# A linear-attention retrieval stage: features repeated by TensorE matmuls instead of 32 SBUF copies

## The chip, the cores and the metric

One NeuronCore of one Trainium2 chip runs the whole kernel. The metric is the device time of one execution in microseconds (us), from the first to the last instruction of that core and what lies around them. Before the change it is 643.27 us, the median of 3 runs (642.25 to 644.81).

## What is computed

The kernel is a two-layer network over 1024 tokens (32 sequences of 32) with 256 features: attention, gated networks with adapters, and in the second layer a retrieval from banks of memories, paged attention and a mixture of experts. The change lies in the retrieval (`_L1_attn_ref` in the reference), cut here to what is kept of it:

```python
sigma_q = elu(q) + 1                      # q = hidden @ Wq.T, 16 heads of 16 features
a_unnorm = einsum('bhsd,nhde->nbhse', sigma_q, memories)      # 4 banks n
norm     = einsum('bhsd,nhd->nbhs', sigma_q, memory_norms)
a = a_unnorm / clip(norm, 1e-6)[..., None] * active[n]
combined = einsum('nbhse,hn->bhse', a, softmax(bank_weights))
out = combined @ Wo.T                     # added to x
```

The kernel divides first and then multiplies by the memories: for every head, bank and token there is one share, softmax weight times active over norm. The features of a pair of heads (32 rows), repeated for 4 banks (128 rows), are multiplied by their shares, and one matmul with 128 rows of memories sums over banks and features at once.

## The kernel before, around the retrieval

All activations are kept features by tokens: two chunks `c` of 128 features, 1024 tokens in two halves `n` of 512 columns. There is no scheduler. Each engine has a list of instructions written out by hand (`lin_tensor`, `lin_vector`, `lin_scalar`, and SP's list of DMAs), which it takes in order, and semaphores are what one waits for of another. The retrieval stands between the second attention (`att_b`) and the paged attention (`page_*`).

1. TensorE projects `yT` with `lin_wq` into PSUM banks 4 to 7 (L1093); VectorE and ScalarE make `sig` = elu + 1 of it (L1154, L1191, L1147), four blocks (c, n).
2. SP issues 32 DMAs (L1883), each of which copies 32 rows of `sig` over 1024 tokens, 128 KB, to one of four row groups of `sig4`, so that `sig4[:, i]` holds head pair i four times. The 16 of chunk 0 signal `lin_rep0`, those of chunk 1 `lin_rep1`.
3. TensorE makes the norms: 64 rows (4 banks of 16 heads) for each half (L1099). VectorE clips, inverts and scales them on 64 partitions, one half after the other (L1161, L1163, L1166). ScalarE makes a high part of them for the fast fp32r format (L1195), VectorE the rest (L1168).
4. For 16 units (pair i, half n), TensorE spreads the shares from 64 rows to 128 with a 0/1 matrix `sel_r`, two fp32r matmuls a unit (L1117) into four rotating banks; VectorE multiplies by `sig4` into `sigq`, a ring of eight buffers (L1175); after each four units TensorE multiplies by the memories, four matmuls of 32 output rows each (`memories`, L1107), and ScalarE keeps the result as `comb` (L1198).
5. TensorE projects with `lin_wo` (L1127) and VectorE adds into `xT` (L1180). `page_tensor` waits for the four of these (`lin_out` >= 4), and VectorE's part of the page stage stands behind them in its list.

Meanwhile GpSimd gathers 40 blocks of the cache by indirect DMA (L1920), with nothing of the retrieval in its list. SP, after the 32 copies, waits for the last L1175 (`lin_scaled` >= 16), loads the experts' weights of 6.5 MB into `wbig`, over `sig4` (L1886), and then stores the new keys and values (`new_kv`, L1890), for which GpSimd's second series of gathers waits.

A matmul of fp32 operands is in the trace two records, each of which streams the columns twice; one of fp32r operands is one record.

## Time and profile before

| | us |
|---|---|
| median of the runs (lowest, highest) | 643.27 (642.25, 644.81) |
| span of the profiled execution | 644.2 |
| TensorE busy with matmuls | 508.7 |
| VectorE busy | 372.4 |
| retrieval, from the first L1093 to the first matmul of the page stage | 72.8 (328.46 to 401.26) |

The profiled execution is one run; its span is 0.9 us (0.14%) over the median, within the spread of the runs, so differences worked out in it are taken off the median as they are. In the rows, "start us, us" are the start from the beginning of the span and the length of a merged stretch, `x8` the number of instructions in it, and the bracket tells how long the engine was idle before and what released it. "Remote" as a releaser means that the signal came at a time at which no instruction of the trace ended. A granted clock (PEclk) of 1.00 is TensorE's 2.4 GHz, 0.50 is 1.2 GHz.

### The profile page before, as it was taken

How to read it: one execution, taken by the hardware profiler on the slowest of the kernel's cores; microseconds unless marked ns; L12 is line 12 of the kernel's file. 1: busy time of each engine (PE TensorE's matmuls, PEld its weight loads, DVE VectorE, ACT ScalarE, POOL GpSimd, SP SyncE). 2: the span in 40 equal slices, each digit the busy share in tenths (PEclk: the TensorE clock that was granted, in tenths of full speed). 3: DMA queues.
4: the chain of work that ended last, by engine and by line, in shares of the span. 5: the costliest groups of instructions: out<-in, count | busy, mean ns of one | idle time of the engine just before them, and what ended most of it. 6: DMA issues, size and time to landing. Idle time of an engine off the chain costs nothing.

```text
span 644.2 us, 10575 instructions
## 1 busy us (share of the span) xinstructions
PE 508.7 (79%) x4069; PEld 369.7 (57%) x4069; DVE 372.4 (58%) x784; ACT 235.2 (37%) x510; POOL 268.1 (42%) x248
## 2 busy tenths in 40 slices
PE   2978799999998999998775519737889896169975
PEld 1445458886886878666432204625667565068865
DVE  2736667886786887647647205975567564223321
ACT  6024854442433333325820000543456441024330
POOL 4013735463442333145647740088661102715560
PEclk9979699999998999998697558957989787669997
DMA  4990044000000000010029826611010000298416
GB/s 155 404 389 4 2 135 122 1 1 1 0 1 0 1 1 1 1 52 2 1 67 240 216 65 245 236 39 26 16 27 1 3 1 21 103 301 268 135 59 196
DMA packets 26337, 57.00 MB, mean 88 GB/s; under 512 B 4829, under 2 KB 17298, under 8 KB 25392
## 3 DMA queue, kind: packets, MB, share of 16 engines
q1 hardware_dynamic: 19936, 45.06, 20.6%
q0 software_dynamic: 6352, 11.26, 6.2%
q8 instruction: 33, 0.54, 0.3%
q14 instruction: 16, 0.13, 0.1%
HBM read 45.28 MB, written 12.37 MB: 90 GB/s over the span
## 4 chain that ended last, share of the span: by engine, by line
PE 29%; DVE 7%; issue 7%; POOL 3%; another core or an unknown queue 3%; DMA 2%; ACT 1%; DVEq 0%; SPq 0%; POOLq 0%; ACTq 0%
PE ps L1708 4%; PE ps L1322 4%; POOL sorted L1790 2%; PE ps L1716 2%; PE ps L1319 2%; PE ps L1332 1%; PE ps L1381 1%; PE ps L1734 1%; PE ps L403 1%; DVE work L1270 1%; PE ps L1093 1%; PE ps L1127 1%; PE ps L1697 1%; PE ps L691 1%
## 5 line engine op out<-in xcount | busy, mean ns | idle before, releaser
L691 PE MATMUL ps<-x_split,gate_up_split 128*128 128x512 f32 x408 | 103.0, 396 | 0.5 <-ACT work L1802 0.5
L691 PEld LDWEIGHTS ps<-x_split,gate_up_split 128*128 128x128 f32 x408 | 77.3, 190 | 19.1 <-issue 2.4
L884 POOL TENSOR_TENSOR gate_up_split<-wbig,gate_up_split 128x768 fp32r<-128x768 f32 (+1 forms) x25 | 44.5, 1781 | 67.1 <-ACT gate_up_split L824 66.8
L1920 POOL DMA_INDIRECT work<-new_kv,prepi x40 | 43.3, 1081 | 49.0 <-DMA new_kv<-work 37.9
L890 POOL TENSOR_TENSOR down_split<-wbig,down_split 128x384 fp32r<-128x384 f32 (+1 forms) x25 | 29.4, 1175 | 58.3 <-ACT down_split L831 58.3
L715 PE MATMUL ps<-hidden_split,down_split 128*128 128x512 f32 x168 | 46.5, 407 | 8.6 <-ACT hidden_split L873 6.9
L873 ACT ACTIVATE hidden_split<-work 128x512 fp32r<-128x512 f32 x34 | 21.4, 631 | 72.4 <-DVE work L801 72.4
L1920 POOL DMA_INDIRECT work<-in_cache_dram,prepi x40 | 38.5, 962 | 20.1 <-issue 11.9
L1793 POOL DMA_INDIRECT chosen<-work x31 | 30.6, 987 | 33.2 <-ACT work L1779 19.9
L806 DVE TENSOR_TENSOR hidden_split<-work,hidden_split 128x512 fp32r<-128x512 f32 x34 | 29.9, 880 | 23.1 <-ACT hidden_split L873 23.1
L715 PEld LDWEIGHTS ps<-hidden_split,down_split 128*128 128x128 f32 x168 | 32.2, 194 | 17.7 <-issue 10.7
L595 POOL TENSOR_TENSOR work<-work,prep 128x512 f32<-128x512 f32 x16 | 16.8, 1048 | 56.7 <-DVE prep L481 56.0
L1117 PE MATMUL ps<-shares_split,select 64*128 64x512 f32 x32 | 14.2, 614 | 29.3 <-issue 15.7
L1505 ACT ACTIVATE wmid<-ps,prep 128x160 f32<-128x160 f32 x64 | 24.6, 390 | 25.0 <-DVE prep L1404 16.7
L393 PE MATMUL ps<-work 128*32 128x128 f32 x512 | 24.4, 357 | 8.4 <-ACT work L556 8.4
L556 ACT ACTIVATE work<-work 32x512 f32<-32x512 f32 x48 | 29.9, 624 | 0.9
L1117 PEld LDWEIGHTS ps<-shares_split,select 64*128 64x128 f32 x32 | 9.2, 302 | 36.5 <-issue 34.3
L1790 POOL DMA_INDIRECT sorted<-work,prepi x16 | 16.0, 1001 | 33.2 <-DVE prepi L1661 28.6
L801 DVE TENSOR_TENSOR work<-ps,work 128x512 f32<-128x512 f32 x34 | 23.2, 682 | 11.4 <-PE ps L696 7.5
L1322 PE MATMUL ps<-work 128*128 128x160 f32 x128 | 29.6, 360 | 0.0
L393 PEld LDWEIGHTS ps<-work 128*32 128x32 f32 x512 | 19.5, 138 | 15.3 <-ACT work L556 14.6
L1697 PE MATMUL ps<-small,work 128*128 128x128 f32 x62 | 12.4, 287 | 19.4 <-DMA work<-sorted 19.4
(309 smaller groups left out, 1165.5 us busy)
## 6 DMA issues: line engine op xcount, KB each, us to landing
wbig<-in_wE_dram SPq DMA_DIRECT2D x1, 6528.0 KB, 19.2
wbig<-in_wF_dram SPq DMA_DIRECT2D x1, 4992.0 KB, 21.2
wbig<-work SPq DMA_DIRECT2D x32, 128.0 KB
sorted<-wmid SPq DMA_DIRECT2D x1, 3999.0 KB, 15.5
wbig<-in_wG_dram SPq DMA_DIRECT2D x1, 3072.0 KB, 28.1
work<-in_wE_dram SPq DMA_DIRECT2D x6, 384.0 KB
work<-chosen SPq DMA_DIRECT2D x8, 256.0 KB, 4.7
work<-sorted SPq DMA_DIRECT2D x1, 1935.0 KB, 12.9
```

The costliest lines, as they stand in the source:

```text
L393: mm = nc.tensor.matmul(ps[32 * pr:32 * pr + 32, g % 2, c * P:(c + 1) * P], vpar[:, g, a, 4 * c + pr, :], pdiag[:, g % 2, 4 * pr + 2 * c + ...
L556: nc.scalar.activation(pdiag[q, g % 2, :, q], scor[q, g % 4, :].rearrange("p (h k) -> p h k", h=NH), ACT.Copy).then_inc(s("placed"), 1)
L691: mm = nc.tensor.matmul(o, gus[:, w % 2, a, 2 * m + k, :], xs[:, b, k, n * HALF:(n + 1) * HALF], start=(k == 0 and a == b), stop=(k == KC ...
L715: nc.tensor.matmul(o, dns[:, w % 2, a, c], hs[:, i % 2, 0, :], start=(p == 0 and a == 0), stop=False)
L806: nc.vector.tensor_tensor(hs[:, i % 2, 1, :], hid[:, i % 3, :], hs[:, i % 2, 0, :].bitcast(F32), ALU.subtract).then_inc(s("h_lo"), 1)
L884: nc.gpsimd.tensor_tensor(gus[:, k % 2, 1, 0:self.gu_chunks], self.gate_up[:, :, j * P:(j + 1) * P], gus[:, k % 2, 0, 0:self.gu_chunks].bi ...
L890: nc.gpsimd.tensor_tensor(dns[:, k % 2, 1, 0:self.dn_cols], self.down[:, j, :], dns[:, k % 2, 0, 0:self.dn_cols].bitcast(F32), ALU.subtrac ...
L1322: mm = nc.tensor.matmul(ps[:, 2 + b % 2, a * NKEY:(a + 1) * NKEY], qmask[:, b, 2 * a:2 * a + 2, :, :].rearrange("p g h t -> p (g h t)"), k ...
L1708: mm = nc.tensor.matmul(ps[:, t % 2, m * P:(m + 1) * P], tile_w(t)[:, (2 * m + k) * P:(2 * m + k + 1) * P], x_turned[:, t % 2, k * P:(k + ...
L1790: send(sorted_d, by(placei[:, c, g:g + 1]), rows_of[c][:, g, :], None).then_inc(sem("sent"), 16)
L1793: send(chosen_d, by(tile_x(t)[:, D + 1:ROW]), y_tile[:, t % 8, :], None, bounds_check=2 * T - 1, oob_is_err=False)\
L1920: return nc.gpsimd.indirect_dma_start(dst, None, table, bass.IndirectOffsetOnAxis(ap=rows.bitcast(U32), axis=0), **({} if bound is None el ...
```

## The change

**Features.** The 32 DMAs go. TensorE multiplies 32 rows of `sig` with 32 rows of the constant `token` (1 where row and column agree modulo 32), which gives them four times on 128 rows. A batch (`repeat`, L1097 of the new file) is one block (c, n): four such matmuls, on four row groups of the array (rows 0-31, 32-63, ...), into PSUM banks 0 to 3. ScalarE copies each bank into `sig4` (L1216, 16 copies). From the second batch on each matmul waits for the copy out of its bank.

**Shares.** The norms of both halves go to the 128 partitions of one bank (L1105), and the heads stand in another order, so that the shares of chunk c and half n are 32 rows. VectorE clips, inverts and scales them in one pass. They stay fp32: the split into two fp32r parts goes, with ScalarE's rounding of `select` ahead of `att_b`. The units go in pairs (c = 0 and 1 of one r): `spread` is two fp32 matmuls of 32 rows on two row groups (L1121) into two of the banks 5, 6, 0, 1; one semaphore count stands for a pair, and a pair waits for VectorE to be done with the pair before the last.

**Order.** All of half 0 goes first. `memories(n)` takes eight matmuls at once, and the projection of half 0 stands between the spreads of half 1. `sigq` has 16 buffers instead of 8. The constant `sel` has 512 columns instead of 1024. SP's load of the experts' weights waits for the last `memories` as well.

What TensorE's list is from the first projection to the page stage, before (L1093 projects, L1099 norms, L1117 spreads, L1107 memories, L1127 projects):

```order
L1093 MATMUL ps<-work,wmid 128x512 x8
L1099 MATMUL ps<-work,wmid 64x512 x4
L1117 MATMUL ps<-shares_split,select 128x512 x16
L1107 MATMUL ps<-work,wmid 32x512 x4
L1117 MATMUL ps<-shares_split,select 128x512 x8
L1107 MATMUL ps<-work,wmid 32x512 x4
L1117 MATMUL ps<-shares_split,select 128x512 x8
L1107 MATMUL ps<-work,wmid 32x512 x8
L1127 MATMUL ps<-work,wmid 128x512 x8
```

And after, for the same stretch (L1097 repeats, L1105 norms, L1121 spreads, L1131 memories, L1139 projects):

```order
L1085 MATMUL ps<-work,wmid 128x512 x8
L1097 MATMUL ps<-work,small 128x512 x4
L1105 MATMUL ps<-work,wmid 64x512 x4
L1097 MATMUL ps<-work,small 128x512 x12
L1121 MATMUL ps<-work,small 128x512 x10
L1131 MATMUL ps<-work,wmid 32x512 x8
L1121 MATMUL ps<-work,small 128x512 x2
L1139 MATMUL ps<-work,wmid 128x512 x4
L1121 MATMUL ps<-work,small 128x512 x4
L1131 MATMUL ps<-wbig,wmid 32x512 x8
L1139 MATMUL ps<-work,wmid 128x512 x4
```

The repeating of batches 1 to 3 stands ahead of every spread, and each spread, fp32r and twice before, is now one fp32 matmul.

ScalarE's list for the retrieval, with the semaphores that each waits for, before:

```order
L1185 ACTIVATE prep<-prep 64x4 [waits prep_step]
L1186 ACTIVATE prep<-prep 64x1
L1191 ACTIVATE work<-work 128x512 [waits lin_neg] x2
L1191 ACTIVATE work<-work 128x512 [waits lin_sig,lin_neg] x2
L1195 ACTIVATE shares_split<-work 64x512 [waits lin_scale] x2
L1198 ACTIVATE work<-ps 128x512 [waits lin_mem] x4
```

And after:

```order
L1205 ACTIVATE prep<-prep 128x4 [waits prep_step]
L1206 ACTIVATE prep<-prep 128x1
L1211 ACTIVATE work<-work 128x512 [waits lin_neg] x2
L1211 ACTIVATE work<-work 128x512 [waits lin_sig,lin_neg] x2
L1216 ACTIVATE wbig<-ps 128x512 [waits lin_repeated,ffn_down_done]
L1216 ACTIVATE wbig<-ps 128x512 x3
L1216 ACTIVATE wbig<-ps 128x512 [waits lin_repeated]
L1216 ACTIVATE wbig<-ps 128x512 x3
...
L1220 ACTIVATE work<-ps 128x512 [waits lin_mem] x4
```

The copies stand between the exponentials (L1211) and the keeping of the retrieved values (L1220), in four batches.

The diff, cut to its core (left out are the constants' new layout, the widening of slices from 64 to 128 partitions, and lines that only go):

```diff
-        sigq = [cut(work, a + i * HALF, HALF) for a in (6144, 0) for i in range(4)]
+        sigq = [cut(t, a + i * HALF, HALF) for t, a, n in ((work, 6144, 4), (work, 0, 4), (wbig, NH // 2 * T, 8)) for i in range(n)]
         sig4 = cut(wbig, 0, NH // 2 * T).rearrange("p (i t) -> p i t", i=NH // 2)
         comb = cut(work, 8192, 2048).rearrange("p (c t) -> p c t", c=KC)
         neg = cut(work, 0, 1024).rearrange("p (r t) -> p r t", r=2)
         expo = cut(work, 1024, 1024).rearrange("p (r t) -> p r t", r=2)
-        rnorm = work[0:NBANK * NH, 10240:11264]
-        sel_r = split_buf("select", wmid_at, 0, 1024).rearrange("p (i o) -> p i o", i=NH // 2)
-        rnorms = split_buf("shares_split", work_at, 2048, 2048).rearrange("p (s t) -> p s t", s=2)
+        share = cut(work, 10240, HALF)
...
-        PAIRS = [(4 * c + r, n) for c, n in BATCH for r in range(4)]
+        PAIRS = [(c, r, n) for n in range(2) for r in range(4) for c in range(KC)]
+        UNIT_AT = {unit: u for u, unit in enumerate(PAIRS)}
...
+            def repeat(b):
+
+                c, n = BATCH[b]
+                pe.wait_ge(sem("lin_sig"), LIN.index((c, n)) + 1)
+                for r in range(4):
+                    if b:
+                        pe.wait_ge(sem("lin_rep"), 4 * (b - 1) + r + 1)
+                    q = slice(32 * r, 32 * r + 32)
+                    mm = nc.tensor.matmul(ps[:, r, :], const("token")[q, :], sig[q, c, n * HALF:(n + 1) * HALF],
+                                          start=True, stop=True)
+                mm.then_inc(sem("lin_repeated"), 1)
+
+            repeat(0)
             pe.wait_ge(sem("lin_sig"), 4)
-            for n in range(2):
+            for c in range(KC):
+                for n in range(2):
+                    mm = nc.tensor.matmul(ps[64 * n:64 * n + 64, 4, :], nrc[:, c, :], sig[:, c, n * HALF:(n + 1) * HALF],
+                                          start=(c == 0), stop=(c == KC - 1))
+            mm.then_inc(sem("lin_norm"), 1)
+            for b in range(1, 4):
+                repeat(b)
+
+            def spread(n, r):
+
+                pe.wait_ge(sem("lin_scale"), 1)
+                u = 2 * (4 * n + r)
+                if u >= 4:
+                    pe.wait_ge(sem("lin_scaled"), u - 2)
+                elif u == 2:
+                    pe.wait_ge(sem("lin_rep"), 16)
                 for c in range(KC):
-                    mm = nc.tensor.matmul(ps[0:NBANK * NH, n, :], nrc[:, c, :], sig[:, c, n * HALF:(n + 1) * HALF],
-                                          start=(c == 0), stop=(c == KC - 1))
-                mm.then_inc(sem("lin_norm"), 1)
-
-            def memories(b):
-                c, n = BATCH[b]
-                pe.wait_ge(sem("lin_scaled"), 4 * b + 4)
-                for r in range(4):
-                    mm = nc.tensor.matmul(ps[32 * r:32 * r + 32, 2 * c + n, :], pairs[:, 4 * c + r, :],
-                                          sigq[(4 * b + r) % 8], start=True, stop=True)
-                mm.then_inc(sem("lin_mem"), 1)
-
-            pe.wait_ge(sem("sel_ready"), 1)
-            for u, (i, n) in enumerate(PAIRS):
-                pe.wait_ge(sem("lin_share"), n + 1)
-                if u >= 4:
-                    pe.wait_ge(sem("lin_scaled"), u - 3)
-                for part in range(2):
-                    mm = nc.tensor.matmul(ps[:, 4 + u % 4, :], sel_r[0:NBANK * NH, i, :],
-                                          rnorms[0:NBANK * NH, part, n * HALF:(n + 1) * HALF],
-                                          start=(part == 0), stop=(part == 1))
+                    q = slice(64 * n + 32 * c, 64 * n + 32 * c + 32)
+                    mm = nc.tensor.matmul(ps[:, (5, 6, 0, 1)[(u + c) % 4], :], const("sel")[q, r * P:(r + 1) * P], share[q, :],
+                                          start=True, stop=True)
                 mm.then_inc(sem("lin_spread"), 1)
...
+            def memories(n):
+                pe.wait_ge(sem("lin_scaled"), 8 * n + 8)
+                if n:
+                    pe.wait_ge(sem("lin_comb"), 2)
+                for c in range(KC):
+                    for r in range(4):
+                        mm = nc.tensor.matmul(ps[32 * r:32 * r + 32, (4, 7)[c], :], pairs[:, 4 * c + r, :],
+                                              sigq[UNIT_AT[c, r, n]], start=True, stop=True)
+                    mm.then_inc(sem("lin_mem"), 1)
+
+            def project(n):
                 pe.wait_ge(sem("lin_comb"), 2 * n + 2)
-                for k in range(KC):
-                    mm = nc.tensor.matmul(ps[:, 4 + u, :], lin_wo[:, k, c * P:(c + 1) * P],
-                                          comb[:, k, n * HALF:(n + 1) * HALF], start=(k == 0), stop=(k == KC - 1))
-                mm.then_inc(sem("lin_proj"), 1)
+                for c in range(KC):
+                    for k in range(KC):
+                        mm = nc.tensor.matmul(ps[:, 2 + c, :], lin_wo[:, k, c * P:(c + 1) * P],
+                                              comb[:, k, n * HALF:(n + 1) * HALF], start=(k == 0), stop=(k == KC - 1))
+                    mm.then_inc(sem("lin_proj"), 1)
+
+            for r in range(4):
+                spread(0, r)
+            spread(1, 0)
+            memories(0)
+            spread(1, 1)
+            project(0)
+            spread(1, 2)
+            spread(1, 3)
+            memories(1)
+            pe.wait_ge(sem("lin_out"), 2)
+            project(1)
...
+            dve.wait_ge(sem("lin_norm"), 1)
+            nc.vector.tensor_scalar(share, ps[:, 4, :], 1e-6, None, ALU.max).then_inc(sem("lin_inv"), 1)
+            dve.wait_ge(sem("lin_inv"), 1)
+            nc.vector.reciprocal(share, share).then_inc(sem("lin_inv"), 1)
+            dve.wait_ge(sem("lin_inv"), 2)
+            dve.wait_ge(sem("lin_coef"), 5)
+            nc.vector.tensor_scalar(share, share, coef[:, :], None, ALU.mult).then_inc(sem("lin_scale"), 1)
+
+            def keep_projection(n):
+                for c in range(KC):
+                    dve.wait_ge(sem("lin_proj"), 2 * n + c + 1)
+                    to = xT[:, c, n * HALF:(n + 1) * HALF]
+                    nc.vector.tensor_tensor(to, ps[:, 2 + c, :], to, ALU.add).then_inc(sem("lin_out"), 1)
+
+            for u, (c, r, n) in enumerate(PAIRS):
+                dve.wait_ge(sem("lin_spread"), u // 2 + 1)
+                dve.wait_ge(sem("lin_rep"), 4 * BATCH.index((c, n)) + r + 1)
+                nc.vector.tensor_tensor(sigq[u], ps[:, (5, 6, 0, 1)[u % 4], :], sig4[:, 4 * c + r, n * HALF:(n + 1) * HALF],
                                         ALU.mult).then_inc(sem("lin_scaled"), 1)
-            for u, (c, n) in enumerate(BATCH):
-                dve.wait_ge(sem("lin_proj"), u + 1)
-                to = xT[:, c, n * HALF:(n + 1) * HALF]
-                nc.vector.tensor_tensor(to, ps[:, 4 + u, :], to, ALU.add).then_inc(sem("lin_out"), 1)
+            keep_projection(0)
+            keep_projection(1)
...
-                nc.scalar.activation(rnorms[nb, 0, h], rnorm[:, h], ACT.Copy).then_inc(sem("lin_hi"), 1)
+            act.wait_ge(sem("ffn_down_done"), ffn_b.count("down_done", 16))
+            for b, (c, n) in enumerate(BATCH):
+                act.wait_ge(sem("lin_repeated"), b + 1)
+                for r in range(4):
+                    nc.scalar.activation(sig4[:, 4 * c + r, n * HALF:(n + 1) * HALF], ps[:, r, :], ACT.Copy)\
+                        .then_inc(sem("lin_rep"), 1)
             for u, (c, n) in enumerate(BATCH):
                 act.wait_ge(sem("lin_mem"), u + 1)
-                nc.scalar.activation(comb[:, c, n * HALF:(n + 1) * HALF], ps[:, 2 * c + n, :],
+                nc.scalar.activation(comb[:, c, n * HALF:(n + 1) * HALF], ps[:, (4, 7)[c], :],
                                      ACT.Copy).then_inc(sem("lin_comb"), 1)
...
-            for c in range(KC):
-                sp.wait_ge(sem("lin_sig"), 2 * c + 2)
-                for r in range(4):
-                    for m in range(NBANK):
-                        sp.dma_start(sig4[32 * m:32 * m + 32, 4 * c + r, :], sig[32 * r:32 * r + 32, c, :])\
-                            .then_inc(sem(f"lin_rep{c}"), 16)
             sp.wait_ge(sem("lin_scaled"), len(PAIRS))
+            sp.wait_ge(sem("lin_mem"), 4)
...
-            nc.scalar.activation(sel_r[nb].rearrange("p i o -> p (i o)"), const("sel")[nb], ACT.Copy)\
-                .then_inc(sem("sel_ready"), 1)
```

## Rows read from the trace of the kernel before

**Rows 1.** The page: span, and the experts' weights (DMA issues, us to landing).

```profile
span 644.2 us, 10575 instructions
...
wbig<-in_wE_dram SPq DMA_DIRECT2D x1, 6528.0 KB, 19.2
```

**Rows 2.** Timeline of TensorE, 328 to 391 us: start, us, engine, line, operation.

```profile
328.46 7.11 PE L1093 MATMUL ps<-work,wmid 128*128 128x512 f32 x16 [0.88 <-DVE work L506]
337.73 5.34 PE L1099 MATMUL ps<-work,wmid 128*64 128x512 f32 x8 [2.17 <-DVE work L1147]
347.31 2.95 PE L1117 MATMUL ps<-shares_split,select 64*128 64x512 f32 x8 [4.24 <-issue]
353.80 3.75 PE L1117 MATMUL ps<-shares_split,select 64*128 64x512 f32 x8 [3.54 <-issue]
357.48 1.93 PE L1107 MATMUL ps<-work,wmid 128*32 128x512 f32 x8
...
386.56 3.75 PE L1117 MATMUL ps<-shares_split,select 64*128 64x512 f32 x8 [13.59 <-DVE work L1175]
```

**Rows 3.** Timeline of VectorE, 336 to 401 us.

```profile
336.21 1.47 DVE L1147 SCALAR_TENSOR_TENSOR work<-ps,work 128x512 f32<-128x512 f32 x2
341.21 0.68 DVE L1161 TENSOR_SCALAR work<-ps 64x512 f32<-64x512 f32 x1 [3.53 <-issue]
341.93 3.35 DVE L1163 RECIPROCAL work<-work 64x512 f32<-64x512 f32 x1
345.31 0.48 DVE L1166 TENSOR_SCALAR work<-work,prep 64x512 f32<-64x512 f32 x1
...
352.98 2.47 DVE L1175 TENSOR_TENSOR work<-ps,wbig 128x512 f32<-128x512 f32 x4
366.52 2.48 DVE L1175 TENSOR_TENSOR work<-ps,wbig 128x512 f32<-128x512 f32 x4 [11.07 <-DMA wbig<-work]
385.73 4.46 DVE L1175 TENSOR_TENSOR work<-ps,wbig 128x512 f32<-128x512 f32 x7 [16.72 <-remote]
...
400.43 0.69 DVE L1180 TENSOR_TENSOR xT<-ps,xT 128x512 f32<-128x512 f32 x1 [1.02 <-PE ps L1127]
```

**Rows 4.** Timeline of SP's DMA issues, 300 to 460 us.

```profile
335.20 29.44 SPq L1883 DMA_DIRECT2D wbig<-work  x32
391.07 0.38 SPq L1886 DMA_DIRECT2D wbig<-in_wE_dram  x1
409.44 4.06 SPq L1890 DMA_DIRECT2D new_kv<-work  x2
```

**Rows 5.** Timeline of ScalarE: the last exponential, the first retrieved values kept.

```profile
336.33 0.63 ACT L1191 ACTIVATE work<-work 128x512 f32<-128x512 f32 x1 [1.09 <-DVE work L1154]
...
384.31 0.60 ACT L1198 ACTIVATE work<-ps 128x512 f32<-128x512 f32 x1 [31.97 <-remote]
```

**Rows 6.** Timelines of TensorE and VectorE near the kernel's start.

```profile
10.12 1.93 PE L2057 MATMUL ps<-work 32*32 32x256 f32 x16 [0.49 <-DMA work<-in_mix_table_dram,prepi]
...
14.92 0.76 DVE L2006 BATCH_NORM_STATS2 prep<-ps 128x6 f32<-128x256 f32 x2 [4.10 <-remote]
```

**Rows 7.** Stretches of TensorE: length, busy (instructions), granted clock, DMA share, GB/s.

```profile
332.00:335.60 3.60, 3.56 (x9) 1.00 0.34 98
...
353.80:357.50 3.70, 3.70 (x12) 0.50 1.05 255
...
373.00:386.50 13.50, 0.00 (x0) 0.50 0.21 58
...
390.20:393.30 3.10, 3.10 (x18) 0.61 0.33 45
```

**Rows 8.** Start of paged attention: GpSimd's last cache gather, its first overlay, TensorE.

```profile
378.00 0.95 POOL L1920 DMA_INDIRECT work<-in_cache_dram,prepi  x1 [0.30 <-issue]
416.87 1.50 POOL L1920 DMA_INDIRECT work<-new_kv,prepi  x1 [37.91 <-DMA new_kv<-work]
...
431.45 1.12 PE L1311 MATMUL ps<-small,work 128*128 128x128 f32 x4 [3.30 <-DVE work L1398]
```

71 lines of the change are left out of this document (18 added, 53 removed).

## The prediction, made before the changed kernel had run

> **What bounds the kernel now.** I read the timeline of each engine through the retrieval and ask of each gap who ends it. TensorE projects at full clock until about 335.6 us [rows 2, 7]; `sig` is complete at 337.68 [rows 3]. From there to the last addition into `xT`, which ends at 401.12 (400.43 + 0.69) [rows 3], 63.4 us pass, and TensorE is mostly idle in them: the first four units of shares are spread at 347.31, the last at 386.56 after a gap of 13.59 [rows 2]. The reader is to see in [rows 3] what VectorE waits for: the multiplication L1175 waits 11.07 us for the copies `wbig<-work`, until 366.52, and then 16.72 us, from 369.0 to 385.73, for something marked remote. The copies are issued from 335.20 over 29.44 us [rows 4], and the DMA engines are full meanwhile (share 1.05) [rows 7], so the first wait is theirs.
>
> The second is odd. ScalarE's L1198 starts at 384.31 [rows 5], but L1107, whose result it keeps, has ended at 357.48 + 1.93 = 359.41 [rows 2]: TensorE's signal reaches ScalarE and VectorE 24.9 us late. No copy is left then, and the DMA engines are mostly idle (share 0.21) [rows 7]. The trace shows one more such case: near the start L2057 ends at 12.05 and VectorE starts at 14.92 [rows 6], while GpSimd gathers and SP loads a block of weights. What both have in common is indirect gathers beside large plain transfers. Signals of TensorE in times of gathers alone are prompt (L1099's first half to L1161 at 341.21 [rows 2, 3]). So I put this wait down to the copies too, with less certainty, and keep it for the rivals.
>
> The price of what the change puts on TensorE depends on the clock: from 353.80 to 357.50 it is busy all the time and granted 0.50, its 1.2 GHz, and it rises only within 390.20 to 393.30 (mean 0.61, so at about 392.6) [rows 7], some 6 us after an unbroken run of matmuls began at 386.56 [rows 2].
>
> **Prices.** An fp32 matmul of 512 columns on the whole array costs 0.89 at full clock: 8 in 7.11 [rows 2]. At half clock the four of L1107, on four column groups, take 1.93 together [rows 2]: what one costs, 1.71 and a drain of 0.2. For row groups the nearest row is L2057, two sets of four tiles on four row groups, 256 columns each, in 1.93 [rows 6], where eight in a row would take about 7. I call one such group a set and take 0.89 or 1.71 for it, with a drain of 0.15 or 0.2. No row shows 128 output columns in four banks; the other bound is four in a row, 3.55 or 6.8.
>
> The Trainium skill (TensorE: Matmul & The Clock Gate, section "Part 3: Packing small matmuls") gives 3.07 times, not four, for four row groups of 512 columns. By that a repeating batch costs a third more and the sum 1 to 2 us more; [rows 6] stand nearer to four.
>
> A VectorE operation from PSUM takes 0.68 alone and 0.62 in a row (four in 2.47) [rows 3]; ScalarE's copy takes 0.60 alone [rows 5], and I take 0.58 in a row. From one engine's end to the next one's start I take 0.13: L1175's first ends at 353.67, the matmul starts at 353.80 [rows 2, 3].
>
> **Removed.** The 32 copies and their waits. L1099's four sets (5.34, while the clock falls) [rows 2] become two, as the halves lie on two column groups. Clip, inverse and scaling (0.68 + 3.35 + 0.48) happen once instead of twice; rounding and subtraction go. 128 partitions cost what 64 cost: 0.68 for L1161 as for L1175 [rows 3]. Shares, complete after 352 before, are ready at 344.8 (norms 337.8 to 340.2, then 0.1 + 4.5). This is hidden: the repeating takes longer. The rounding of `select` ahead of the attention and the smaller load of constants are off the path: nothing.
>
> **Added: repeating, on the path.** Batch 0 runs behind the first projection, 335.6 to 336.6. ScalarE is free at 336.96 [rows 5]; its four copies end at 339.3. The norms hold TensorE until 340.0. Then a loop: the last matmul of a batch waits for the fourth copy of the batch before, takes 1.91 at half clock, and four copies follow, 2.32; with two hand-overs 4.45 per batch. Batch 1 is copied at 344.3, batch 2 at 348.8, batch 3 at 353.2. TensorE's spreads stand behind all of it in its list, the second pair needs all 16 copies, and VectorE waits for the spreads.
>
> The Trainium skill (TensorEngine Tiling (Array Packing), section "PSUM Bottleneck") says that the PSUM copy may become the bound after such a speedup, and to use ScalarE and VectorE both. Here one engine copies.
>
> **Changed: spreads, memories, projections.** A pair of spreads is one set, at half clock 1.71, more than VectorE's 1.24 for two units, so TensorE works without a break from 353.4: four pairs to 360.2. By what happened after 386.56 the clock is back at about 359.5. The rest at full clock: memories of half 0, two sets, to 362.0; kept by ScalarE and handed over, 363.0; projection of half 0, four sets, to 366.5; two pairs and VectorE's last multiplications, to 370.1; memories of half 1, to 372.0; kept, 372.9; projection of half 1, to 376.7; addition, 377.5. The spreads in all cost about what they did: 3.75 for eight fp32r matmuls (four units) [rows 2] against two sets, 3.42.
>
> **Sum.** The stage ends at 377.5 instead of 401.12, 23.6 us earlier, and the page stage behind it is released by that. The profiled execution would span 644.2 - 23.6 = 620.6 [rows 1]. Its span is 0.9 over the median, so the median goes from 643.3 to 619.7; I say 620.
>
> **What is late next.** SP loads the experts' weights after the last memories, at 372.1 instead of 391.07 [rows 4], which takes 19.2 [rows 1]: to about 393, as GpSimd's cache gathers run until 379 [rows 8] beside it. The stores of `new_kv` come 8.3 and 12 us after the stage (409.44, 3.7 apart) [rows 4], at 386 and 390, behind the weights in one queue, and land at about 395. GpSimd's overlays then start 2 us later than the shift (416.87) [rows 8]. TensorE takes the first of them at 431.45, released by VectorE, 14.6 after they begin [rows 8]; five of them, at 1.5 and a pause, take 9. So I cost it at nothing; without that slack, 3.
>
> **Rivals.**
> 1. *Clock stays full.* The loop is 3.45 instead of 4.45, and the first pairs are shorter: end at 372.7, time 615. Against it: pieces of 3.7 us at half clock did not lift it before [rows 7].
> 2. *Clock stays half*, as 32 rows with waits don't lift it: projections +7.1, memories and last pairs +5.2. End 389.9, time 632. For it: spreads of 64 rows ran at 0.50 [rows 7].
> 3. *Row groups don't overlap.* A batch costs 6.8 but hides part of the copies; the clock returns as forecast. End 392, time 634. With the clock at half as well: end 417, time 659, slower.
> 4. *Late signal, once.* From 372.1 the weights' load runs beside the last gathers, as both late signals had it. If the signal of the last memories comes as then, 5.4 after the last gather's end at 378.95 [rows 5, 8], the stage ends at 389.6, time 632.
> 5. *Slower than before: the late signal belongs to the gathers alone.* Then a tiled matmul of the retrieval is not reported before 384.3, as before. If it is the first batch, everything from 336.6 on follows it: 384.3 + 40.9 = 425, 24 later, time 667. It decides from how early in the 41 us the late one falls: with 17 us of the stage or less behind it, it is no slower. Against it: L1099's prompt signal, and none late while gathers run from 416.87 on.
> 6. *Weights before new keys*, not hidden: 623.
>
> **How the numbers follow.** Forecast 0.50 (own range 616 to 624: imperfect overlap of row groups, and where the clock rises), rivals: 1 0.10; 2 0.10; 3 0.05, with half clock 0.02; 4 0.13; 5 0.06; 6 0.04. Low is 613, a little under rival 1; high is 634, which takes in 2, 3 and 4. 0.5%, some 3 us, is what a measurement can tell from no change. Faster 0.92, of which the slower cases are no part; slower 0.07; 0.01 for one that ends between.
>
> **What the profile of after would show.** A batch of L1097 in 1.9 or 1.0 us; 3.5 or 7 speaks for rival 3. L1216 in four stretches of 2.3, from about 337, 342, 346.5 and 351. The granted clock from 353 to 377. Every wait on TensorE ending within 0.2 of its last record; a remote wait means rivals 4 or 5. The last addition at 377, SP's load at 372. I am wrong if the stage ends before 374 or after 382, or if the time behind it changes by over 3 us.

## The result: slower by 2%, and the profile after

The changed kernel takes 656.05 us (median of 4 runs, 651.72 to 659.58) where the kernel before takes 643.86 (4 runs, 642.25 to 644.81): ratio 1.020, 95% interval 1.015 to 1.025. The prediction was 620, range 613 to 634. Times are medians; one slow execution of e18 below, 628.67 us where its fastest took 617.75, is left out of its median.

The page of the changed kernel, its span and the line of TensorE, which was busy for 508.7 us before:

```profile
span 653.7 us, 10616 instructions
...
PE 511.0 (78%) x4101; PEld 370.2 (57%) x4101; DVE 367.6 (56%) x779; ACT 240.9 (37%) x523; POOL 266.5 (41%) x248
```

The span grew by 9.5 us. The retrieval, from the first L1085 at 328.18 to the first matmul of the page stage at 411.09, lasts 82.9 us, against 72.8 (328.46 to 401.26) before: 10.1 more; ahead of the stage and behind it 0.3 us each are saved. TensorE's timeline in the changed kernel, which answers to [rows 2] (L1097 repeats, L1105 norms, L1121 spreads, L1131 memories, L1139 projects):

```profile
328.18 7.11 PE L1085 MATMUL ps<-work,wmid 128*128 128x512 f32 x16 [0.88 <-DVE work L500]
335.21 1.14 PE L1097 MATMUL ps<-work,small 32*128 32x512 f32 x8
337.45 1.94 PE L1105 MATMUL ps<-work,wmid 128*64 128x512 f32 x8 [1.10 <-DVE work L1170]
339.32 1.14 PE L1097 MATMUL ps<-work,small 32*128 32x512 f32 x8
348.06 3.44 PE L1097 MATMUL ps<-work,small 32*128 32x512 f32 x8 [7.60 <-issue]
362.80 2.59 PE L1097 MATMUL ps<-work,small 32*128 32x512 f32 x6 [11.29 <-issue]
...
383.86 7.68 PE L1121 MATMUL ps<-work,small 32*128 32x512 f32 x16 [16.89 <-ACT wbig L1216]
391.47 3.64 PE L1131 MATMUL ps<-work,wmid 128*32 128x512 f32 x16
```

A batch of four row groups costs 1.14 us at full clock, so the row groups overlap. Between the batches, and ahead of the later spreads, TensorE does nothing for 7.6, 11.3 and 16.9 us. It waits for ScalarE's copies out of PSUM, and ScalarE's timeline says what those wait for:

```profile
336.58 2.04 ACT L1216 ACTIVATE wbig<-ps 128x512 f32<-128x512 f32 x4
347.32 2.06 ACT L1216 ACTIVATE wbig<-ps 128x512 f32<-128x512 f32 x4 [8.70 <-remote]
362.06 2.06 ACT L1216 ACTIVATE wbig<-ps 128x512 f32<-128x512 f32 x4 [12.67 <-remote]
381.65 2.06 ACT L1216 ACTIVATE wbig<-ps 128x512 f32<-128x512 f32 x4 [17.53 <-remote]
```

Read the two views against each other. The second batch ends at 339.32 + 1.14 = 340.46 and its copies start at 347.32, 6.9 us later; the third ends at 351.50, copies at 362.06, 10.6 later; the fourth ends at 365.19 + 1.06 = 366.25, copies at 381.65, 15.4 later. That is the "remote" wait of [rows 3, 5], three times over. The trace has the changes of the semaphore of these batches too: at 347.30, 362.03 and 381.62, each 0.03 us or less ahead of the copies. So it is TensorE's signal that comes late, and not ScalarE that is slow to take it. VectorE has the same, against the spread that ends at 366.97:

```profile
384.48 1.29 DVE L1198 TENSOR_TENSOR work<-ps,wbig 128x512 f32<-128x512 f32 x2 [38.89 <-remote]
...
410.25 0.69 DVE L1193 TENSOR_TENSOR xT<-ps,xT 128x512 f32<-128x512 f32 x1 [1.02 <-PE ps L1139]
```

In the other direction nothing is late: the copies end at 383.71, and TensorE is at work at 383.86. GpSimd's cache gathers run from 328.31, one every 1.25 us, and the last ends at 378.21, 3.4 and 6.3 us ahead of the last two late signals (timeline of GpSimd, answering to [rows 8]):

```profile
377.27 0.94 POOL L1937 DMA_INDIRECT work<-in_cache_dram,prepi  x1 [0.30 <-issue]
428.70 1.61 POOL L1937 DMA_INDIRECT work<-new_kv,prepi  x1 [50.48 <-DMA new_kv<-work]
```

The 32 copies are gone here, and the load of the weights comes at 405.84, behind it all. So neither can make these signals late.

### The profile page after: what moved, and what is told of

It is laid out like the page before. It is cut to its first block, busy times and chain, and to the rows that moved or that the text cites. A ratio compares the mean times of both kernels' runs of the same rounds, so it can differ in the third digit from the quotient of the medians.

```text
span 653.7 us, 10616 instructions
## 1 busy us (share of the span) xinstructions
PE 511.0 (78%) x4101; PEld 370.2 (57%) x4101; DVE 367.6 (56%) x779; ACT 240.9 (37%) x523; POOL 266.5 (41%) x248
## 4 chain that ended last, share of the span: by engine, by line
PE 29%; issue 8%; another core or an unknown queue 6%; DVE 4%; ACT 3%; DMA 1%; POOL 1%; POOLq 0%; SPq 0%; DVEq 0%; ACTq 0%
PE ps L1730 5%; PE ps L1344 4%; PE ps L1738 2%; PE ps L1341 2%; PE ps L1121 2%; PE ps L1756 1%; PE ps L1354 1%; PE ps L397 1%; ACT wbig L1216 1%; DVE work L1292 1%; PE ps L1139 1%; PE ps L1403 1%; PE ps L1719 1%; PE ps L685 1%
## 5 line engine op out<-in xcount | busy, mean ns | idle before, releaser
L709 PE MATMUL ps<-hidden_split,down_split 128*128 128x512 f32 x168 | 46.6, 407 | 8.6 <-ACT hidden_split L867 7.0
L1344 PE MATMUL ps<-work 128*128 128x160 f32 x128 | 31.5, 378 | 0.0
L1198 DVE TENSOR_TENSOR work<-ps,wbig 128x512 f32<-128x512 f32 x8 | 5.2, 686 | 40.3 <-remote 38.9
L1793 ACT ACTIVATE work<-ps 128x128 f32<-128x128 f32 x31 | 8.6, 277 | 49.5 <-PE ps L1730 48.2
## 6 DMA issues: line engine op xcount, KB each, us to landing
wbig<-in_wF_dram SPq DMA_DIRECT2D x1, 4992.0 KB, 20.3
```

The costliest lines, as they stand in the source:

```text
L709: nc.tensor.matmul(o, dns[:, w % 2, a, c], hs[:, i % 2, 0, :], start=(p == 0 and a == 0), stop=False)
L1344: mm = nc.tensor.matmul(ps[:, 2 + b % 2, a * NKEY:(a + 1) * NKEY], qmask[:, b, 2 * a:2 * a + 2, :, :].rearrange("p g h t -> p (g h t)"), k ...
```

## Experiments

The stage is always from the first projection of the retrieval to the first matmul of the page stage. The records number the chips: e1 to e4 ran on chip 13, e5 to e8 on chip 8, e9 to e18 on chip 1. All times, the result's too, are of executions that were recorded. e1 to e4, e7, e8 and e10 to e14 are one execution each. e7, e8, e11 to e14, e17 and e18 bring other or fewer rows of the cache than the kernel needs, so they compute something else and serve to measure only.

| kernel | chip | time, us (kernel before beside it) | stage, us |
|---|---|---|---|
| before, changed (the result) | not on record | 643.86, 656.05 | 72.8, 82.9 |
| e1 changed, all gathers late | 13 | 673.2 (648.1) | 48.7 |
| e2 before, all gathers late | 13 | 677.2 (648.1) | 51.7 |
| e3 changed, 20 of 40 late | 13 | 647.2 (648.1) | 62.0 |
| e4 whole-array repeating | 13 | 656.1 (648.1) | 83.4 |
| e5 changed, 8 early, rest mixed | 8 | 628.9 (615.7) | 48.8 |
| e6 before, the same | 8 | 629.2 (615.7) | 51.7 |
| e7 changed, quarter of bytes | 8 | 600.3 (615.7) | 49.0 |
| e8 changed, 32 rows | 8 | 604.5 (615.7) | 48.7 |
| e9 changed | 1 | 657.2 (642.7) | 83.2 |
| e10 before | 1 | 643.2 (642.7) | 73.1 |
| e11 changed, quarter of bytes | 1 | 666.1 (642.7) | 90.3 |
| e12 changed, 32 rows | 1 | 663.9 (642.7) | 89.6 |
| e13 changed, plain, by GpSimd | 1 | 617.9 (645.9) | 48.8 |
| e14 changed, plain, by SyncE | 1 | 622.0 (645.9) | 49.0 |
| e15 changed | 1 | 662.4 (645.9) | 87.4 |
| e16 as e5 | 1 | 654.3 (645.9) | 48.9 |
| e17 before, plain, by GpSimd | 1 | 633.2 (646.7) | 62.2 |
| e18 changed, plain, by GpSimd | 1 | 622.8 (646.7) | 49.0 |

### The gathers moved out of the stage: e1, e2, e3

```diff
# e1 (and e2, in the kernel before)
+            pool.wait_ge(sem("lin_out"), 4)
             for t in order:
                 gather(kv[:, t, :], cache, key_rowi[:, t:t + 1]).then_inc(sem("cached"), 16)
# e3
-            for t in order:
+            for i, t in enumerate(order):
+                if i == 20:
+                    pool.wait_ge(sem("lin_out"), 4)
                 gather(kv[:, t, :], cache, key_rowi[:, t:t + 1]).then_inc(sem("cached"), 16)
```

> The changed kernel, with GpSimd's 40 gathers from the cache held back until the retrieval is over (a wait for lin_out >= 4 ahead of the loop). Theory A (the gathers make TensorE's signals late): every wait of ScalarE and VectorE on TensorE in the retrieval ends within 0.2 us of the last matmul's end, and the last addition into xT is at 376 to 379 us, 33 us before the changed kernel's 410.9. Theory B (matmuls on row or column groups are reported late, whatever else runs): the waits marked remote stay, of 7 to 17 us, and the last addition comes at about 411. The span is no measure here, since 50 us of gathers now stand ahead of the paged attention; by A about 648, by B about 680.

> The kernel before, with the same wait ahead of its 40 gathers. Theory A: the remote wait of 16.7 us on L1175 and the late start of L1198 are gone, the 32 copies have the DMA engines for themselves and land before 360, and the last addition is at 375 to 384 instead of 401. Theory B: the remote wait stays, and the last addition comes at 395 to 401. If the 32 copies themselves make the signals late (theory C), it also stays.

> The changed kernel with 20 gathers where they were (328 to 353) and 20 after the retrieval. Theory A: the late signals end within some 6 us of the 20th gather, so by 360; copies of the second batch at 347 as before, of the third by 360, of the fourth at 364; last addition at 385 to 390. Theory B: last addition at about 411. The span lies between those of the changed kernel and of the one with all gathers late.

e1 takes 673.2 us and e2 677.2. The whole is longer than before, since the pages wait for gathers that start some 50 us later, and by more than the 648 that I had put for e1, since late signals now fall on the pages. What counts is the stage. ScalarE in e1:

```profile
333.72 2.04 ACT L1216 ACTIVATE wbig<-ps 128x512 f32<-128x512 f32 x4
337.67 2.06 ACT L1216 ACTIVATE wbig<-ps 128x512 f32<-128x512 f32 x4 [1.91 <-PE ps L1097]
340.95 2.06 ACT L1216 ACTIVATE wbig<-ps 128x512 f32<-128x512 f32 x4 [1.21 <-PE ps L1097]
345.17 2.07 ACT L1216 ACTIVATE wbig<-ps 128x512 f32<-128x512 f32 x4 [2.16 <-PE ps L1097]
...
391.14 1.02 ACT L1464 ACTIVATE work<-ps 128x1024 f32<-128x1024 f32 x1 [6.47 <-remote]
...
428.30 1.02 ACT L1464 ACTIVATE work<-ps 128x1024 f32<-128x1024 f32 x1 [35.05 <-remote]
```

Every wait on TensorE in the stage is prompt, and the stage lasts 48.7 us instead of 82.9. The last two lines are as telling: behind the stage, where the gathers now run, ScalarE waits "remote" for L1312, a plain matmul on the whole array, whose last one has ended at 388.08. The lateness moved with the gathers. In e2 the copies are all still there, but the copy-bound wait of 11.07 us in [rows 3] has nearly gone. VectorE and SP of e2:

```profile
350.60 2.47 DVE L1175 TENSOR_TENSOR work<-ps,wbig 128x512 f32<-128x512 f32 x4
354.91 2.49 DVE L1175 TENSOR_TENSOR work<-ps,wbig 128x512 f32<-128x512 f32 x4 [1.84 <-DMA wbig<-work]
```

```profile
332.67 20.31 SPq L1883 DMA_DIRECT2D wbig<-work  x32
```

The 32 copies are issued over 20.3 us instead of 29.4 [rows 4], and L1198 starts at 357.10, behind a prompt signal. So most of what [rows 3] show was the gathers' doing, not the copies'. e3 stands between: with 20 gathers in the stage two of three signals are late, the third, behind the last of the 20, is not:

```profile
344.46 2.06 ACT L1216 ACTIVATE wbig<-ps 128x512 f32<-128x512 f32 x4 [8.09 <-remote]
354.32 2.06 ACT L1216 ACTIVATE wbig<-ps 128x512 f32<-128x512 f32 x4 [7.80 <-remote]
358.55 2.06 ACT L1216 ACTIVATE wbig<-ps 128x512 f32<-128x512 f32 x4 [2.16 <-PE ps L1097]
```

### Are tiled matmuls reported late? e4

```diff
-                    q = slice(32 * r, 32 * r + 32)
-                    mm = nc.tensor.matmul(ps[:, r, :], const("token")[q, :], sig[q, c, n * HALF:(n + 1) * HALF],
+                    mm = nc.tensor.matmul(ps[:, r, :], tokens[:, r, :], sig[:, c, n * HALF:(n + 1) * HALF],
...
```

`tokens[:, r]` is `token` with the rows outside group r set to zero; GpSimd makes it ahead of its gathers.

> The changed kernel with its 16 repeating matmuls on the whole array: 128 rows of a 0/1 matrix that is zero outside one row group, made by GpSimd ahead of the attention, instead of 32 rows on a row group; gathers where they were. Four of them cost 3.6 to 6.8 us instead of 1.1 to 3.4. Theory A: signals late as before, waits marked remote on L1216 and on L1198 until 380 to 385, last addition at 410 or later. Theory B: the signals of the repeating batches are prompt, the last copy is done by 365 at the latest, and the last addition comes before 398.

TensorE and ScalarE in e4:

```profile
346.18 6.48 PE L1097 MATMUL ps<-work,wmid 128*128 128x512 f32 x8 [4.68 <-issue]
```

```profile
362.98 2.06 ACT L1217 ACTIVATE wbig<-ps 128x512 f32<-128x512 f32 x4 [15.47 <-remote]
```

The batch of 346.18 ends at 352.66 and is copied at 362.98, 10.3 us late; in the changed kernel it was 10.6. So the form of the matmul is not what makes its signal late. That a batch now takes 6.4 us costs nothing, since it fits into time lost anyway.

### Gathers mixed with the overlays: e5, e6, e16

Only 8 gathers run ahead of the pause; each group of 5 later ones follows the overlay of the group four before it, on semaphores of their own.

```diff
-            for t in order:
-                gather(kv[:, t, :], cache, key_rowi[:, t:t + 1]).then_inc(sem("cached"), 16)
-            pool.wait_ge(sem("cached"), 16 * NGT)
+            def cache_rows(n):
+                if n == 8:
+                    pool.wait_ge(sem("lin_out"), 4)
+                t = order[n]
+                gather(kv[:, t, :], cache, key_rowi[:, t:t + 1]).then_inc(sem(f"cached{n // 5 % 4}"), 16)
+
+            for n in range(20):
+                cache_rows(n)
...
+                if n % 5 == 0:
+                    pool.wait_ge(sem(f"cached{q4 % 4}"), 16 * 5 * (q4 // 4 + 1))
...
+                if n % 5 == 4 and n < 20:
+                    for m in range(n + 16, n + 21):
+                        cache_rows(m)
```

> Theory A (TensorE's signals reach ACT and DVE late only while GpSimd's row gathers are under way, so they should be kept out of the stage's round trips and then cost the pages nothing): 8 gathers run at the stage's start, the other 12 of the first four groups behind the stage, and each later group of 5 cache rows right behind the overlay of the group four before it. The stage is between 49 us (all gathers behind it, measured) and 62 us (20 gathers in it, measured), about 50. The overlays start when the new keys have landed, about 18 us behind the stage, instead of also waiting for all 40 cache rows. Against 656 us for the changed kernel: 33 us from the stage, and the pages start about 28 us earlier but their groups come every 12 us of GpSimd's time instead of every 6: 620 us, between 612 and 632, so 3 to 4% faster than the kernel before. Theory D (the gathers only move the loss: late signals then fall on the page projections and on the rotations, as L1464's 6.47 us did where all 40 ran behind the stage, and the pages wait for GpSimd): 635 to 650.

> The same new order of the gathers in the kernel before, so that the change itself (matrix instead of copies) is compared where no gather disturbs it. Theory A: the stage shortens from 72.7 us to about 53 (51.5 was measured with no gather in it), and this kernel is 3 to 4 us slower than the changed kernel with the same order: about 624 us if that one is at 620. Theory F (the change itself is a loss, whatever the gathers do): as fast as that one or faster.

> The kernel of e5 (8 gathers in the stage, the others mixed with the overlays) on another chip: it took 629 us where the kernel before took 616. If its gathers lie where late signals cost nothing, it takes 625 to 635 us on a chip where the kernel before takes about 645 too, and is then 2% faster there; if late signals catch the page projections and rotations instead, 640 to 655.

The stage is about what was expected, 48.8 and 51.7, with no late signal. The times are not: e5 takes 628.93 us (4 runs, 628.51 to 631.13) and not 620, and the kernel before took only 615.66 beside it (7 runs, 613.38 to 617.13), 27 to 32 us less than on the other chips. And e6 takes 629.17 (628.73 to 632.11). The mixing itself, e6 against the kernel before, is therefore a loss of 2.4% there (interval 2.0 to 2.9), and the 3.0 us that the changed kernel gains in the stage are given back. GpSimd in e5, then in e6:

```profile
395.66 1.02 POOL L1937 DMA_INDIRECT work<-new_kv,prepi  x1 [4.43 <-DMA new_kv<-work]
```

```profile
394.78 1.90 POOL L1920 DMA_INDIRECT work<-new_kv,prepi  x1 [0.30 <-issue]
```

The overlays start no earlier in e5. Its stores of the new keys go out at 382.33 and are awaited until 395.66, 13.3 us; in e6 they go out at 385.58, and the overlays start 9.2 us later, as soon as GpSimd has done its gathers. In e5 the load of the experts' weights, issued at 368.90 and landing 22.4 us later, still lies ahead of them in SP's queue.

On chip 1 the same kernel (e16) takes 654.31 (4 runs, 652.51 to 656.01), 1.4% more than before (interval 0.8 to 1.9). Its stage is 48.9 us, 38 us shorter than that of the changed kernel beside it (e15), but the total is shorter by only 8 us. ScalarE's and VectorE's waits from 390 to 530 us in e16, then VectorE's in e5 (us in total, times, longest):

```profile
ACT wmid L1499 <- remote: 12.0, 1, 12.0
ACT work L1515 <- remote: 10.5, 4, 5.9
```

```profile
DVE prep L1426 <- remote: 21.6, 2, 15.0
```

```profile
DVE prep L1426 <- PE ps L1344: 22.5, 17, 6.1
```

The late signals fall on the pages instead, with waits of up to 15 us each, where e5 had none. On this chip moving gathers moves the loss.

### Another chip, and what about a gather matters: e7 to e12, e15

```diff
# e7, e11: 64 floats of a row
-                gather(kv[:, t, :], cache, key_rowi[:, t:t + 1]).then_inc(sem("cached"), 16)
+                gather(kv[:, t, 0:64], cache.rearrange("n (a f) -> (n a) f", a=4), key_rowi[:, t:t + 1]).then_inc(sem("cached"), 16)
# e8, e12: 32 rows
+                gather(kv[0:32, t, :], cache, key_rowi[0:32, t:t + 1]).then_inc(sem("cached"), 16)
```

e9, e10 and e15 are the changed kernel, the kernel before and the changed kernel, unedited.

> The changed kernel, but each of the 40 cache gathers brings 64 of a row's 256 floats (other rows than meant, so what it computes differs): as many gathers, as many rows, a quarter of the bytes. If the lateness goes with the bytes moved (theory A-bytes), the four waits of the copies at L1216 behind TensorE shrink from 0, 8.7, 12.7 and 17.5 us to under 5 each, and the stage from 82.8 us to under 60. If it goes with the number of gathers or of their rows (theory A-count), the waits and the stage stay within some 10% of those, at 75 to 85 us.

> The changed kernel, but each of the 40 cache gathers brings 32 rows of full width and not 128 (the other rows stay unloaded, so what it computes differs): as many gather instructions, a quarter of the rows and of the bytes. If the number of rows (one descriptor each) sets the lateness, it shrinks with them: stage under 60 us instead of 82.8, whatever the run with a quarter of the bytes does. If the gather instructions on GpSimd set it, whatever they move, the stage stays at 75 to 85 us.

> The changed kernel as it is, on whichever chip this call gets, since the kernel before itself took 616 us on the chip of the call before and 644 to 648 on the two before that. Theory G (how late TensorE's signals come while the row gathers run differs from chip to chip): where the kernel before takes about 616 us, its stage has no late signal, the waits of the copies at L1216 are about 2 us each, the stage lasts 49 us and the changed kernel takes 609 to 614, a gain of 2 to 7 us as the stages of e1 and e2 differ by 3; where the kernel before takes about 645, the changed one takes about 656 again, ratio 1.015 to 1.025. Theory H (the chips differ in something else, and the late signals are the same everywhere): ratio 1.015 to 1.025 on either chip.

> The kernel before as it is, beside the changed one on the same chip, for its trace. Theory G: at about 616 us the copy at L1198 behind the four matmuls waits about 7 us on TensorE and not 32, and the stage lasts 51 to 53 us and not 72.7; at about 645 it waits over 25 us. Theory H: the wait is over 25 us whatever the time.

> The changed kernel with gathers of 64 floats a row instead of 256 (what it computes differs), on the same chip as the changed kernel itself. On a chip with late signals: under 60 us of stage if the lateness goes with the bytes, 75 to 85 us if it goes with the number of gathers or rows. On a chip without: stage 49 us, and a time below the changed kernel's only by what the shorter gathers save behind the stage.

> The changed kernel with gathers of 32 rows instead of 128 (what it computes differs), on the same chip. On a chip with late signals: under 60 us of stage if the number of rows (or their bytes) sets the lateness, 75 to 85 us if the number of gather instructions does. On a chip without: stage 49 us.

> The changed kernel once more, on the chip of this call. Theory G (the lateness goes with the chip): where the kernel before takes about 645 us, ratio 1.015 to 1.025 again; where it takes about 616, 609 to 614 us, as its stage is 3 us shorter than the one of before when no signal is late (48.6 against 51.5 in e1 and e2, 48.7 against 51.6 in e5 and e6).

On chip 8 e7 and e8 have no late signal. On chip 1 the same two kernels are the slowest of all. The third batch's copies in e7 and in e11, one kernel on two chips; then the second's in e12:

```profile
339.90 2.06 ACT L1216 ACTIVATE wbig<-ps 128x512 f32<-128x512 f32 x4 [1.21 <-PE ps L1097]
```

```profile
370.19 2.06 ACT L1216 ACTIVATE wbig<-ps 128x512 f32<-128x512 f32 x4 [17.53 <-remote]
```

```profile
375.10 2.06 ACT L1216 ACTIVATE wbig<-ps 128x512 f32<-128x512 f32 x4 [35.70 <-remote]
```

So a quarter of the bytes, or of the rows, lessens nothing on chip 1 (stages of 90.3 and 89.6 us, over the 85 that I had at most): what is left unchanged in both is 40 indirect transfers, one every 1.2 us. Whether they disturb goes with the chip. On chip 1 the changed kernel itself gives 1.022 (e9, interval 1.019 to 1.025; 657.24 against 642.69) and 1.028 (e15, 1.022 to 1.034, the ratio over the 1.025 that I had at most), and the kernel before shows its long wait again, in e10 (VectorE waits twice there, 3.89 and 10.61 us):

```profile
383.73 1.09 ACT L1198 ACTIVATE work<-ps 128x512 f32<-128x512 f32 x2 [33.88 <-remote]
```

The changed kernel itself never met a chip like 8; e7 and e8, which differ from it only in lighter gathers, are 11 to 15 us under the kernel before there. One more thing goes with the late signals. The trace keeps a record of each change of a semaphore; counted between 300 and 380 us there are 834 in e7 (chip 8) and 235 in e11 (chip 1), for the same kernel. What is missing is mostly the landings of the gathers themselves, 16 changes each: 640 of them in e7, 124 in e11. Of the other changes there are 194 and 111. And records go missing ahead of the lateness: e16 has 59 of the 128 landings of its first 8 gathers, and no signal in its stage is more than 0.4 us late.

### Indirect or plain, GpSimd or SyncE: e13, e14

```diff
# e13 (e18; e17 in the kernel before)
-                gather(kv[:, t, :], cache, key_rowi[:, t:t + 1]).then_inc(sem("cached"), 16)
+                nc.gpsimd.dma_start(kv[:, t, :], cache[t % 8 * P:(t % 8 + 1) * P, :]).then_inc(sem("cached"), 16)
# e14: the same transfers in SP's list, behind the load of wP
+            sp.wait_ge(sem("att_out"), 2 * ATT_TOTAL["out"])
+            for t in range(NGT):
+                sp.dma_start(kv[:, t, :], cache[t % 8 * P:(t % 8 + 1) * P, :]).then_inc(sem("cached"), 16)
... (and GpSimd's loop of 40 gathers goes)
```

> The changed kernel with 40 plain transfers issued by GpSimd (128 rows of the cache in a row) in place of the 40 cache gathers, so what it computes differs: GpSimd still issues 40 transfers into the same queue and as many land, but no row is looked up. Theory A-gather (the gather instruction on GpSimd makes the signals late): no wait over 3 us at L1216, stage 49 us. Theory A-queue (every transfer that GpSimd issues does, or its landing): on a chip where the kernel before takes about 645 us the waits at L1216 stay at 7 to 18 us and the stage at 75 to 90. Where it takes about 616 us, 49 us by both.

> The same 40 plain transfers, issued on SyncE's queue instead of GpSimd's, at about the same time (what it computes differs). If transfers and their landings as such make TensorE's signals late, the stage stays at 75 us or more on a chip where the kernel before takes about 645; if GpSimd has to be in it, the stage is 49 to 52 us on either kind of chip, and the pages start at least 15 us earlier.

GpSimd and ScalarE in e13, on chip 1:

```profile
323.92 21.64 POOL L1957 DMA_DIRECT2D work<-in_cache_dram  x40 [8.26 <-DVE work L500]
```

```profile
336.12 2.06 ACT L1216 ACTIVATE wbig<-ps 128x512 f32<-128x512 f32 x4 [1.91 <-PE ps L1097]
339.39 2.07 ACT L1216 ACTIVATE wbig<-ps 128x512 f32<-128x512 f32 x4 [1.21 <-PE ps L1097]
```

Forty transfers of 128 KB, issued by the same engine, twice as densely, and signalling the same semaphore: no signal is late, and 837 semaphore changes are recorded between 300 and 380 us, as on chip 8. The stage is 48.8 us and the kernel takes 617.86. GpSimd's queue carried the same in both, packets and MB, in the changed kernel and in e13:

```profile
q0 software_dynamic: 6352, 11.26, 5.7%
q0 software_dynamic: 6352, 11.26, 5.9%
```

From SyncE it is no different (49.0). So neither the bytes, nor the queue, nor the landings make TensorE's signals late, on the chips that show it, but the series of indirect gathers that GpSimd works off.

Not every series does. The 40 overlays behind the stage are indirect gathers of GpSimd too, sixteen of them issued within 23 us, yet in the changed kernel the longest "remote" wait from 411 to 520 us is this one of ScalarE:

```profile
452.68 0.60 ACT L1515 ACTIVATE work<-ps 128x512 f32<-128x512 f32 x1 [1.96 <-remote]
```

They read `new_kv`, with a bound on the row number. In e1, where they follow 2.5 us behind the 40 cache gathers, signals are late while they alone run: TensorE's L1321 ends at 434.20 and 440.72, and ScalarE's L1491 for the two halves starts at 452.15 and 464.78. What a series must have to do this is open.

### What the change is worth without late signals: e17 against e18

> The kernel before with the 40 plain transfers from GpSimd in place of the cache gathers (what it computes differs), against e18, which is the changed kernel with the same: the change itself, with no gather in the stage. On either kind of chip: no signal late in the stage, its length 51.5 us as in e2, and 620 to 625 us in all on a chip where the kernel before takes about 645, since e18's kernel took 617.9 there. If the change is worth what its stage says, this one is 2 to 4 us slower than e18; if the shorter stage is given back behind it, within 1 us.

> The changed kernel with 40 plain transfers from GpSimd in place of the cache gathers (the kernel of e13), timed on the same chip as e17: 616 to 620 us where the kernel before takes about 645, stage 48.7 us, and 2 to 4 us (0.3 to 0.7%) under e17. The prediction's own sum for that difference, were the kernel before's long wait left out, is 51.5 less 49.0, 2.5 us. If it is over e17, the changed code costs more than it saves even where no signal is late.

e17 takes 633.16 us (6 runs, 630.86 to 634.55), e18 622.81 (5 runs, 617.75 to 625.30): 10.3 us less, ratio of the medians 0.984, no run of one within the other's. My expectation of 2 to 4 us was wrong, as e17's stage is 62.2 us and not 51.5. VectorE in e17:

```profile
356.49 2.48 DVE L1175 TENSOR_TENSOR work<-ps,wbig 128x512 f32<-128x512 f32 x4 [5.04 <-DMA wbig<-work]
367.66 4.46 DVE L1175 TENSOR_TENSOR work<-ps,wbig 128x512 f32<-128x512 f32 x7 [8.69 <-DMA wbig<-work]
```

Forty transfers beside the 32 copies hold the copies up, 13.7 us of waiting where e2 had 1.8. That is what the change saves: little where the copies have the DMA engines to themselves (3.0 us, e1 against e2), 13.2 us of the stage where they don't. Some 3 us of the 13.2 are lost again behind the stage.

## Why the prediction was wrong

**The new stage, right.** From the first projection to the end of the last addition the sum gave 49.0 us (328.46 to 377.5). Without gathers e1 gives 373.19 + 0.69 - 325.32 = 48.6. Its parts: a batch was put at 1.91 at half clock, with 0.89 and a drain of 0.15 at full clock; the first two took 1.14, the third 2.50 spread over its waits and the fourth, at half clock, 3.45. Four copies were put at 2.32 and take 2.06. (The terms of the loop, 1.91, 2.32 and two hand-overs of 0.13, make 4.49 and not 4.45, which changes nothing.) The last copies end 21.9 us into the stage, not 24.7. The spreads took 7.3 instead of 6.8. TensorE's granted clock by stretch in e1:

```profile
338.40:341.00 2.60, 2.50 (x8) 1.00 0.00 0
341.60:345.90 4.30, 4.17 (x12) 0.50 0.00 0
347.40:354.70 7.30, 7.30 (x20) 0.50 0.01 3
359.40:363.10 3.70, 3.70 (x12) 1.00 0.00 0
```

The clock falls two batches later than I assumed and comes back between 29.4 and 34.1 us into the stage, where I had 31.0. Rivals 1 to 3 are out: row groups overlap (1.14 us a batch), and the clock neither stays full nor half. The Trainium skill's 3.07 times for four row groups (TensorE: Matmul & The Clock Gate, section "Part 3: Packing small matmuls") would make a batch 3.55 / 3.07 = 1.16, an estimate worked out from the 3.55 of the prediction; the trace agrees with it, and my four times, 1.04 with the drain, was a little low. Its remark that the PSUM copy may become the bound (TensorEngine Tiling (Array Packing), section "PSUM Bottleneck") agrees with the trace too: 2.06 us of copies for 1.14 of matmuls.

**The step that failed** is "So I put this wait down to the copies too": the remote wait of [rows 3, 5]. It belonged to the gathers. In the sum it stands as the hand-over of 0.13 us from a batch to its copies, which took 6.9, 10.6 and 15.4. What I called odd, that no copy was left and the DMA engines mostly idle (0.21) [rows 7] while the signal was out, spoke against the copies, and I let one row near the kernel's start, with gathers and a large load together, outweigh it. I dismissed the gathers because L1099's signal at 341.21 was prompt "in times of gathers alone". That was misread: the copies were being issued from 335.20 [rows 4], so the row speaks against the copies as much as against the gathers. The runs show why it was prompt: the lateness needs a series. 8 gathers in the stage make no signal more than 0.4 us late (e16). In the changed kernel the signal after the start of the seventh is prompt; that of the norms, after the ninth, is 1.6 us late (339.39 to 340.99), the one after the tenth 6.9, and then 10.6, 15.4 and 17.5. The number is not sharp, for the prompt one at 341.21 came after ten, nor does the lag always grow: in e15 it is 9.8, 16.2 and 9.8.

**The wrong case was rival 5**, "the late signal belongs to the gathers alone", held at 0.06. It had the cause and the sign. Its size was off, 667 against 656, since it let one signal wait for the end of the gathers. In e12 it was so: its second batch's signal came at 375.10, behind the last gather's end at 373.24. But in the changed kernel as it is each signal is late by itself, and what counts, by these traces, is how many round trips that begin with TensorE follow one another while gathers run. (The overlays from 416.87 on, which I held against this rival, are the other kind of series, with no wait over 2 us.) Before, the gathers cost the stage 72.8 - 51.7 = 21.1 us: by e17 about 10.5 of it as copies held up by other transfers (62.2 - 51.7) and the other 10.6 as late signals, as far as plain transfers stand for gathers there. After, they cost 82.9 - 48.7 = 34.2, nearly all of it late signals: 6.9 + 10.6 + 15.4 = 32.9 ahead of the copies, and the rest from a slower third batch (3.44 instead of 2.50 in e1) and at the spreads. The change puts three such round trips one behind another into the gathers' time. Before, what TensorE did between its late signals did not wait for the first of them, so they passed as one wait. The L1107 that ended at 359.41 was kept at 384.31 [rows 5], and the one that ended at 372.98 right behind it:

```profile
385.95 0.60 ACT L1198 ACTIVATE work<-ps 128x512 f32<-128x512 f32 x1 [1.04 <-remote]
```

34.2 - 21.1 - 3.0 (the shorter stage) = 10.1, which is the measured difference by the way these terms are formed, not a check of them.

**Behind the stage, right.** The stores of the keys come 8.3 us after the stage's end as before (419.26 - 410.94), the overlays start 9.4 us after the stores instead of 7.4, the 2 us I had for the weights ahead of them, and it costs nothing: the time behind the stage changed by 0.3 us. With earlier overlays, in e5, it does cost the 3 us of rival 6.

**Still open.** Why TensorE's signals are late on chips 13 and 1 and not on chip 8, which was met once. What sets the cache gathers apart from the overlays. Whether recording takes part: every time here is of a recorded execution, and semaphore records are missing in the runs with late signals, so the lateness may be partly the recorder's, and an execution without it could come out otherwise; no run here can tell. The Trainium skill (NOTIFIC — the notification-queue block, section "7.1 Overflow: three behaviours, one of which stalls the engine") says that this block, which writes such records, holds its producers back inside rather than lose a record there, and that a full ring of records can drop new ones. No run here shows that it held an engine back, nor where the missing records were lost. What the changed kernel takes on a chip like 8 was not measured.

None of these kernels that does the whole work beats the kernel before: e3, at 647.19 against 648.10, is the same within what single runs can tell.

## What to carry to other kernels

When a wait ends at a time at which nothing in the trace ends, find what is running in all such cases, and price the change with that cause at its worst: a round trip added between two engines cost up to 15 us here where it fell among the gathers. Try a disturber by moving it out of the stage and watching the stage alone, not the total. And time a doubtful kernel on more than one chip: the kernel before took 616 us on one and 643 to 648 on the others, about as much as the largest change of any experiment here (29 us, e2).

## What was not expected of the hardware

- While the cache gathers run in a series on GpSimd, TensorE's semaphore signals reached ScalarE and VectorE up to 34.5 us late in the stage (e12: a batch ends at 340.57, its copies start at 375.10) and 46.6 behind it (e2: the last L1290 ends at 391.67, ScalarE's L1442 starts at 438.27), those of ScalarE and VectorE to TensorE in the stage came within 0.2 us. Plain transfers of the same size from the same engine did nothing of the kind (e13).
- It was so on chips 13 and 1, and absent on chip 8.
- A second series of 40 indirect gathers, the overlays, left no "remote" wait over 2.0 us in the kernels before and after.
- The size of the gathers does not matter: 128 KB, 32 KB in 128 rows and 32 KB in 32 rows gave stages of 83.2, 90.3 and 89.6 us on chip 1.
- 32 copies of 128 KB inside the SBUF are issued over 20.3 us alone (e2), 22.1 beside 40 plain transfers (e17), but 29.4 beside 40 indirect gathers [rows 4] and 33.3 in e10.
